# A Mamba-like layer on eight cores: another order at the beginning and at the seam of two passes, and y transposed by TensorE instead of by DMA

## The chip, the cores and the metric

The kernel runs on the eight cores of one Trainium2 chip. Each core works on one batch element of u (4096 rows of 1024 numbers); there is no traffic between cores. The metric is the device time of one execution, in microseconds (us), taken on the slowest core; lower is better. The time of a kernel is the median of its runs.

## The reference, cut to what matters

```python
xn = layernorm(x)                                   # 4096 x 1024 per core
zxbcdt = xn @ in_proj_w.T                           # z 2048, x 2048, B 64, C 64, dt 16
# forward branch, and the same backward in time with its own parameters:
dt  = softplus(dt + dt_bias);  A = -exp(A_log)
xBC = silu(causal_conv4(xBC))
y   = scan(h = h * exp(dt*A) + dt*x*B ;  y = h.C) + D * x      # 16 heads of 128
yz  = y * silu(z)
y_dir = yz * rsqrt(mean(yz*yz) + eps) * norm_w
s = (y_fw + y_bw) @ out_proj_w.T
g = silu(quantize6(xn) @ quantize6(ffn_w).T + ffn_bias)        # blocks of 32, fp6 grid
out = x + s * g
```

## The kernel before

**Two passes.** The sequence is cut into 16 groups of 256 rows, each of two chunks of 128 rows. The first pass (A) goes through the groups from the last to the first. For a group it normalizes u (`layer_norm`), transposes the result by DMA (`xt`), projects it with the weights `wx` (x, B, C; nine blocks) and `wz` (z; four blocks), stores these to memory (`sp_x`, `sp_bc`, `sp_z`), convolves, scans backward and stores y (`sp_y`). It also prepares the quantized input of the FFN (`ffn_input`, stored as `sp_xd`), and once per group for eight groups a tile of the quantized FFN weights (`ffn_weight_tile`). The weights `wx` and `wz` lie as float32 in memory and are cast to bfloat16 by DMAs that GpSimd issues into the large tile `ar`. The second pass (B) goes forward: it loads the spilled x, B, C and z, convolves and scans forward, adds the stored y of pass A (`yb`, a part of `ar`, loaded from `sp_y`), transposes the sum into `yt` (a part of `ar` too), multiplies it by the out-projection weights (`wov`, in `ar`, scaled by `nwt`), computes the FFN (`ffn_chunk`) and writes the output (`b_out`). Between the passes, at the **seam**, `ar` changes hands: `wx` makes way for the FFN weights (`wf`), the bias rows (`fbt`) and the buffers of pass B, `wz` for `wov`. The conv weights (`cd`), `nega`, `ddiag`, `dbt` and others are loaded or made anew for the forward direction.

**What sets the order.** The program is recorded as units (`put` for a compute instruction or a bundle of them, `dma` for a transfer), each with an engine, the units it waits for, and a guess of its duration. `Plan.queues` then runs a list schedule over these guesses: whenever an engine is free it takes, of the units that would be ready, the one with the lowest rank (`P.turn`, or `P.rank` where it is set), then the one recorded first. The result is a fixed order of instructions for each engine. On the chip each engine works through its order; an instruction that has to wait holds up all behind it. All DMAs but those that cast are issued by one queue, SP, in such an order too, and there a wait also holds up all transfers behind it.

**Buffers.** The names in brackets are rings: `Ring.take` hands out the next buffer with the units that must be done before. `ub` (two tiles) holds rows of u, `yz` (three) the gated output, `stg` (five) x for the conv, PSUM is cut into `PJ` (two banks for projections), `CV` (one pair of banks for the conv) and `SC` (two pairs, for the scan's products). All helpers that issue an instruction have one line each: 354 for TensorE, 364 for ScalarE, 367 to 378 for VectorE and GpSimd, 381 for DMAs.

**The places that the change touches.** The constants' DMAs are recorded first, `c_ii` and `cw` ahead of u. VectorE then makes `cd` (six instructions), `nega` and `ddiag` (needs `i128` and `dvt`) before it comes to the statistics of u (`bns`). At the seam sixteen VectorE instructions scale `wov` by `nwt`, and the bias is split into three bfloat16 rows through `stmp` and `yz`. In pass B each chunk's sum of y is transposed by

```python
t_yt = dma("sp", f"yt{yi}", go(yt, yz[:].rearrange("p (k f) -> p k f", k=16),
                              transpose=True), [v, yfree], 512, us=2.4, rate=150.0)
```

## Time and profile before

| | us |
|---|---|
| median of 3 runs | 1624.54 (1620.02 to 1625.74) |
| the profiled execution | 1631.24 |
| its span on the slowest core (5) | 1629.4 |
| TensorE busy in it | 1323.2 |
| VectorE busy | 989.5 |
| ScalarE busy | 826.8 |
| GpSimd busy | 703.0 |

The profile is of one execution; its span is that from the first to the last instruction of the slowest core. PE is TensorE, PEld its weight loads, DVE VectorE, ACT ScalarE, POOL GpSimd, SPq the issuing of DMAs. In a line such as `start us, us, engine line op out<-in xcount [idle before <-releaser]` the brackets say how long the engine stood idle just before and what ended it. The window rows give the busy time of each engine in a stretch, the granted TensorE clock (1.00 is 2.4 GHz, 0.50 is 1.2 GHz), the busy share of the 16 DMA engines and what they moved.

### The profile page before, as it was taken

The numbers are of one execution on the slowest core, as the hardware profiler recorded it, in microseconds if no ns is written. First come the engines' busy times: TensorE is split into PE (matmuls) and PEld (weight loads), VectorE is DVE, ScalarE is ACT, GpSimd is POOL, SyncE is SP. The second block draws the span as 40 slices with busy tenths as digits, with TensorE's granted clock in tenths as the row PEclk, the third lists the DMA queues.
The fourth block names the chain that finished last, engine by engine and source line by source line (L and its number), as shares of the span: only waits on it lengthen the run. The fifth ranks groups of instructions, "written<-read, shape, count | busy, mean of one in ns | idle before, by whom it ended". The sixth has DMA issues, their size and how long they took to land.

```text
span 1629.4 us, 38429 instructions; the slowest of 8 cores (1601.5 to 1629.4 us)
## 1 busy us (share of the span) xinstructions
PE 1323.2 (81%) x13568; PEld 768.9 (47%) x13568; DVE 989.5 (61%) x1769; ACT 826.8 (51%) x1652; POOL 703.0 (43%) x949
## 2 busy tenths in 40 slices
PE   0458989687998899989996379898898988898995
PEld 0325656354655565656663244444444444444442
DVE  1614777665778777667755365666556566565652
ACT  0135656464656566656655354554555555555540
POOL 1422646443555355555532234444443444343442
PEclk9989999898999999999997589998898999999998
DMA  9795889989887687875589777988898899899872
GB/s 163 145 162 94 193 189 202 155 185 194 184 187 155 186 188 180 183 157 145 148 214 261 169 141 172 236 200 203 195 218 191 224 198 226 198 226 206 199 168 77
DMA packets 446831, 298.02 MB, mean 183 GB/s; under 512 B 320689, under 2 KB 394929, under 8 KB 445106
## 3 DMA queue, kind: packets, MB, share of 16 engines
q1 hardware_dynamic: 444050, 282.43, 76.0%
q0 software_dynamic: 2592, 13.14, 5.4%
q8 instruction: 110, 1.80, 0.5%
q14 instruction: 79, 0.65, 0.2%
HBM read 152.39 MB, written 84.93 MB: 146 GB/s over the span
## 4 chain that ended last, share of the span: by engine, by line
PE 51%; DMA 18%; ACT 9%; issue 8%; DVE 8%; SPq 4%; POOL 1%; DVEq 0%; ACTq 0%; POOLq 0%
PE ps L354 51%; SPq L381 4%; DMA xtm<-cvx 4%; ACT L364 3%; DMA ar<-yz 2%; DMA dvt<-dvec 2%; DVE yz L367 2%; DMA g<-scr 2%; ACT e L364 2%; DMA ar<-wob 2%; ACT cvx L364 1%; DMA ar<-wz 1%; ACT sq L364 1%; DMA lts<-spl 1%; DMA xt<-xn 1%
## 5 line engine op out<-in xcount | busy, mean ns | idle before, releaser
L354 PE MATMUL ps<-ar,xt 128*128 128x512 bf16 (+1 forms) x1792 | 382.8, 357 | 134.1 <-DMA xt<-xn 62.4
L354 PEld LDWEIGHTS ps<-ar,xt 128*128 128x128 bf16 x1792 | 149.7, 99 | 328.4 <-issue 186.5
L364 ACT ACTIVATE cvx<-ps,cbt 128x256 bf16<-128x256 f32 x512 | 201.1, 475 | 195.1 <-PE ps L354 157.7
L354 PE MATMUL ps<-xt,ar 128*128 128x256 bf16 x2304 | 276.3, 275 | 11.7 <-DMA ar<-wz 4.2
L354 PE MATMUL ps<-ar 128*128 128x512 bf16 x1024 | 258.6, 397 | 14.2 <-ACT e L364 11.1
L367 POOL TENSOR_TENSOR stmp<-st,dec 128x1024 f32<-128x1024 bf16 x64 | 131.0, 2047 | 277.9 <-DVE spl L378 122.9
L354 PEld LDWEIGHTS ps<-xt,ar 128*128 128x128 bf16 x2304 | 220.0, 99 | 56.0 <-issue 25.6
L367 DVE TENSOR_TENSOR yz<-ps,sz 128x1024 bf16<-128x1024 f32 x128 | 154.9, 1220 | 43.3 <-PE ps L354 42.9
L354 PE MATMUL ps<-stg,cd 64*64 64x256 bf16 x4096 | 156.1, 294 | 24.1 <-ACT cvb L364 12.4
L364 ACT ACTIVATE sq<-yz 128x1024 bf16<-128x1024 bf16 x128 | 135.0, 1054 | 74.0 <-DVE yz L367 35.6
L354 PEld LDWEIGHTS ps<-ar 128*128 128x128 bf16 x1024 | 95.2, 101 | 148.0 <-issue 56.5
L372 POOL TENSOR_SCALAR rr<-rr 128x1 f32<-128x1 f32 x384 | 110.3, 292 | 115.2 <-DVE rr L372 92.9
L367 POOL TENSOR_TENSOR bw<-btm,w 128x1024 bf16<-128x1024 bf16 x64 | 124.5, 1947 | 79.5 <-DMA btm<-cvb 67.1
L354 PEld LDWEIGHTS ps<-stg,cd 64*64 64x64 bf16 x4096 | 113.4, 114 | 80.2 <-issue 76.2
L364 ACT ACTIVATE e<-ps 128x1024 bf16<-128x1024 f32 x128 | 129.6, 1018 | 33.1 <-PE ps L354 32.2
L367 DVE TENSOR_TENSOR e<-e,cbm 128x1024 bf16<-128x1024 bf16 x128 | 97.8, 769 | 58.0 <-ACT e L364 57.9
L371 POOL TENSOR_SCALAR u<-u,stats 128x1024 f32<-128x1024 f32 x32 | 96.9, 3029 | 74.6 <-DVE xn L372 57.8
L354 PE MATMUL ps<-xtm,e 128*128 128x128 bf16 x1024 | 89.6, 233 | 45.0 <-DVE sm L367 16.1
L364 ACT ACTIVATE stg<-ps 128x512 bf16<-128x512 f32 x128 | 76.1, 594 | 94.4 <-PE ps L354 94.0
L364 ACT ACTIVATE sz<-ps 128x512 bf16<-128x512 f32 x128 | 76.4, 598 | 92.7 <-PE ps L354 92.5
L367 POOL TENSOR_TENSOR xd<-v,qs 128x1024 bf16<-128x1024 fp8e4 x40 | 81.7, 2044 | 78.4 <-DMA xd<-xd 32.6
L364 ACT ACT_TABLE_LOAD x66 | 84.7, 1283 | 36.4 <-DMA nega<-alog 18.0
(89 smaller groups left out, 1635.8 us busy)
## 6 DMA issues: line engine op xcount, KB each, us to landing
u<-u SPq DMA_DIRECT2D x54, 512.0 KB, 5.0
sp_x<-stg SPq DMA_DIRECT2D x64, 256.0 KB, 2.8
g<-scr SPq DMA_DIRECT2D x64, 256.0 KB, 5.6
sp_z<-sz SPq DMA_DIRECT2D x32, 512.0 KB, 4.4
sp_y<-yz SPq DMA_DIRECT2D x32, 512.0 KB, 4.8
sz<-sp_z SPq DMA_DIRECT2D x32, 512.0 KB, 4.5
ar<-sp_y SPq DMA_DIRECT2D x32, 512.0 KB, 4.6
stg<-sp_x SPq DMA_DIRECT2D x60, 259.0 KB, 4.8
```

The costliest lines, as they stand in the source:

```text
L354: return lambda e: e.matmul(out, lhsT, rhs, start=start, stop=stop)
L364: return lambda e: e.activation(out, in_, func, **kw)
L367: return lambda e: e.tensor_tensor(out, a, b, op=op)
L371: return lambda e: e.tensor_scalar(out, a, s1, None, op0=op0)
L372: return lambda e: e.tensor_scalar(out, a, s1, s2, op0=op0, op1=op1)
L381: return lambda e: e.dma_start(out=out, in_=in_, **kw)
```

## The change

It has three parts.

1. **The beginning.** u is loaded first, then the constants; `wx` waits for the first tile of u; `i128`, `dvt` and `rh` wait for blocks of `wx`; `wz` starts after `wx` block 5; `ddiag` gets a later rank; the second group's projection (`a_front`) is recorded ahead of the first group's z.
2. **The seam.** The FFN weights (`wf`), the constants of pass B and its first `decays` get an earlier turn or rank; the four loads of `wov` come behind the first loads of pass B, each waits for the one before, and ScalarE scales half of the sixteen slices; the bias is split during pass A through a small tile and a DRAM buffer (`fbd`); tiles of the FFN weights are loaded into the third `yz` buffer in pass A (ring `UM`), so that the ring `yz` has two buffers in pass A and three in pass B.
3. **y.** Sixteen transposes by TensorE (a matmul with the identity `i128` in transpose mode, output bfloat16 in a pair of PSUM banks of the ring `SC`) and two copies of 128x1024 by ScalarE take the place of each DMA transpose.

```diff
-    def dma(self, eng, slot, step, after, kb, us=0.5, rate=180.0):
-        land = 2.0 + kb / rate
+    def dma(self, eng, slot, step, after, kb, us=0.5, rate=180.0, lat=None):
+        land = lat or 2.0 + kb / rate
...
-    YZ = Ring("yz", yzb)
+    YZ = Ring("yz", yzb[:2])
+    UM = Ring("um", [yzb[2][:].bitcast(F32)])
...
+    def tr(out, in_, start, stop):
+        return lambda e: e.matmul(out, in_, i128[:], start=start, stop=stop, is_transpose=True)
...
-    k_ii = dma("sp", "k0", go(ii[:], dr["c_ii"]), [], 16)
-    k_cw = dma("sp", "k5", go(cwt[:], dr["cw"][1]), [], 36)
     t_u0 = []
     for i in range(2):
-        t_u0.append(dma("sp", f"u{i}", go(ub[i][:], dr["u"][L - (i + 1) * Q:L - i * Q, :]), [], 512))
+        t_u0.append(dma("sp", f"u{i}", go(ub[i][:], dr["u"][L - (i + 1) * Q:L - i * Q, :]), [], 512,
+                        lat=6.0 + 2 * i))
+    k_ii = dma("sp", "k0", go(ii[:], dr["c_ii"]), [], 16, lat=8.0)
+    k_cw = dma("sp", "k5", go(cwt[:], dr["cw"][1]), [], 36, lat=9.0)
...
-    for b in (8, 0, 1, 2, 3, 4, 5, 6, 7):
-        k_wx[b] = dma("pool", f"wx{b}", go(wxb[b], dr["wx"][b]), [], 1024, us=1.0, rate=130.0)
+    for n, b in enumerate((8, 0, 1, 2, 3, 4, 5, 6, 7)):
+        k_wx[b] = dma("pool", f"wx{b}", go(wxb[b], dr["wx"][b]), [t_u0[0]], 1024, us=0.6,
+                      lat=4.0 + 3.4 * n)
+    k_i = dma("sp", "k4", go(i128[:], dr["c_i128"]), [k_wx[2]], 32, lat=6.0)
+    k_dv = dma("sp", "k9", go(dvt[:], dr["dvec"][1]), [k_wx[2]], 8, lat=7.0)
+    k_rh = [dma("sp", f"k11{i}", go(rhb[i][:], dr["c_rh"][1, i]), [k_wx[4]], 512, lat=9.0)
+            for i in range(2)]
...
-        k_wz.append(dma("pool", f"wz{b}", go(wzb[b], dr["wz"][b]), [k_wx[7], k_wz[b - 1:b]], 2048,
-                        us=1.0, rate=170.0))
+        k_wz.append(dma("pool", f"wz{b}", go(wzb[b], dr["wz"][b]), [k_wx[7 - 2 * (b == 0)], k_wz[b - 1:b]],
+                        2048, us=0.6, lat=9.5))
...
+        P.rank = P.turn + 1.5
         dd = put("dve", tt(
             ddiag[:], i128[:].unsqueeze(1).broadcast_to([128, NH, 128]),
             dvt[:].unsqueeze(2).broadcast_to([128, NH, 128]), ALU.mult),
-            [k_i, k_dv, after], dve1(2048))
+            [k_i, k_dv, after_dd], dve1(2048))
+        P.rank = None
...
     a_conv(NG - 1, fr[NG - 1])
+    P.turn = 0
+    fr[NG - 2] = a_norm(NG - 2)
+
+    P.turn, P.rank = 2, 0.5
+    a_front(NG - 2, fr[NG - 2])
+    P.turn, P.rank = 1, None
     for c in (1, 0):
         a_z(NG - 1, fr[NG - 1], c)
-    P.turn = 0
-    fr[NG - 2] = a_norm(NG - 2)
-    P.turn = 1
...
-    P.turn = 2 * NG + 1
+    P.turn = 2 * NG
...
-        t_wo.append(put("dve", ts(wov[:, k, :], wov[:, k, :], nwt[:, k:k + 1], ALU.mult),
-                        [k_wo[k // 4], k_nw], dve4(1024)))
...
+            si, sp, sfree = SC.take()
+            tp = sp.bitcast(BF16)
+            p = put("pe", [tr(tp[:, k * 128:(k + 1) * 128], yz[:, k * 128:(k + 1) * 128], k % 8 == 0,
+                              k % 8 == 7) for k in range(16)], [v, sfree, k_i], 0.92)
+            t_yt = [put("act", act(yt[:, h * 8:(h + 1) * 8, :],
+                                   tp[:, h * 1024:(h + 1) * 1024].rearrange("p (k t) -> p k t", k=8),
+                                   AF.Copy), [p, yfree], act_us(1024)) for h in range(2)]
+            SC.give(si, t_yt)
+            YZ.give(sc.yz_i, [p])
...
-    base = P.turn + 1
-    P.turn = base
+    base = P.turn
+    P.rank = base - 0.5
     dcs = {0: decays(0, None, t_par, None)}
+    P.rank = None
     P.turn = base + 1
     front = b_front(0)
+    wov = ar[:, WO:WO + 16384].rearrange("p (k m) -> p k m", k=16)
...
+    for b in range(4):
+        k_wo.append(dma("sp", f"wol{b}", go(
+            wov[:, b * 4:(b + 1) * 4, :], dr["wob"][:, b * 4:(b + 1) * 4, :]),
+            [last_a["wz"], wo_casts, front["loads"], k_wo[b - 1:b]], 1024, lat=6.5))
+        for k in range(b * 4, b * 4 + 4):
+            w_ = wov[:, k, :]
+            if k % 2:
+                t_wo.append(put("act", act(w_, w_, AF.Copy, scale=nwt[:, k:k + 1]),
+                                [k_wo[b], k_nw], act_us(1024)))
```

How the planner's order comes out at three places. First VectorE at the very beginning of the program, before (`cd` are the conv weights, `nega` and `ddiag` parameters of the heads, `bns` the statistics of u, `xn` its normalized rows; s_k5, s_k4 and so on are the semaphores of the constants' loads, s_u0 and s_u1 those of u):

```order
L367 TENSOR_TENSOR cd<-ii,cwt 128x768 [waits s_k5,s_k0]
L367 TENSOR_TENSOR cd<-ii,cwt 128x768 x5
L371 TENSOR_SCALAR nega<-nega 128x32 [waits s_act]
L367 TENSOR_TENSOR ddiag<-i128,dvt 128x2048 [waits s_k9,s_k4]
L454 BN_STATS bns<-u0 128x6 [waits s_u0]
L455 BN_STATS bns<-u0 128x6
L454 BN_STATS bns<-u1 128x6 [waits s_u1]
```

and after:

```order
L475 BN_STATS bns<-u0 128x6 [waits s_u0]
L476 BN_STATS bns<-u0 128x6
L477 BN_AGGR stats<-bns 128x2 [waits s_dve]
L475 BN_STATS bns<-u1 128x6 [waits s_u1]
L476 BN_STATS bns<-u1 128x6
L477 BN_AGGR stats<-bns 128x2 [waits s_dve]
L377 TENSOR_SCALAR xn<-u0,stats 128x1024 [waits s_act]
L372 TENSOR_TENSOR cd<-ii,cwt 128x768 [waits s_k5,s_k0]
L372 TENSOR_TENSOR cd<-ii,cwt 128x768 x5
L376 TENSOR_SCALAR nega<-nega 128x32 [waits s_act]
L377 TENSOR_SCALAR xn<-u1,stats 128x1024 [waits s_xt01]
```

The statistics and the first normalization now stand ahead of `cd`, and `ddiag` has left the place in front of them (it is some thirty instructions further down).

Second the DMA queue SP at the seam, from the last store of pass A on (`ar<-wf` and `ar<-wob` load the FFN and out-projection weights, `lts<-spl` is the first link of pass B's decays), before:

```order
L381 DMA cbt<-cb 128x18
L381 DMA ar<-wf 128x8x1024 [waits s_pe]
L381 DMA ar<-wob 128x4096 [waits s_wo3]
L381 DMA sp_z<-sz1 128x2048 [waits s_act]
L381 DMA ar<-wob 128x4096 x3
L381 DMA xt1<-sp_xd 128x1024 x2
L381 DMA rh0<-c_rh 64x2048 [waits s_pe]
```

and after:

```order
L386 DMA ar<-wob 128x4096 [waits s_wol0]
L386 DMA sz0<-sp_z 128x2048 [waits s_dve,s_szs1,s_szs0]
L386 DMA ar<-wob 128x4096 [waits s_wol1]
L386 DMA sbc0<-sp_bc 128x2x259 [waits s_pe]
L386 DMA sz1<-sp_z 128x2048 [waits s_dve]
L386 DMA ar<-wob 128x4096 [waits s_wol2]
L386 DMA_TRANSPOSE btm0<-cvb0 128x2x128 [waits s_act]
L386 DMA_TRANSPOSE lts0<-spl 128x4x128 [waits s_dve]
```

The four loads of `wob` were issued at one go; now the queue itself stands and waits for each before it issues the next, with `lts` behind the fourth. On VectorE the scaling of `wov` stood ahead of the decays of pass B, and now the decays' instructions on `sm0` and `spl` stand ahead of nearly all of it.

Third TensorE in the middle of pass B (`ar,xt1` is the FFN, `ar` alone the out-projection, `rh,lts` the decay weights of the scan, `on3` the bias; s_yt0 is the landing of the DMA transpose), before:

```order
L354 MATMUL ps<-ar,xt1 128x512 [waits s_act]
L354 MATMUL ps<-ar,xt1 128x512 x6
L354 MATMUL ps<-ar,xt1 128x512 [waits s_yt0]
L354 MATMUL ps<-ar,on3 128x512
L354 MATMUL ps<-ar 128x512 x14
L354 MATMUL ps<-ar 128x512 [waits s_act]
```

and after:

```order
L359 MATMUL ps<-i128,yz1 128x128 x12
L359 MATMUL ps<-i128,yz1 128x128 [waits s_act]
...
L356 MATMUL ps<-ar,xt1 128x512 [waits s_act,s_rh01,s_rh00]
...
L356 MATMUL ps<-rh1,lts0 64x512
L356 MATMUL ps<-ar 128x512 x6
L356 MATMUL ps<-ar 128x512 [waits s_dve]
...
L359 MATMUL ps<-i128,yz2 128x128 x12
L359 MATMUL ps<-i128,yz2 128x128 [waits s_act]
```

The transposes of the two chunks (`i128,yz1`, `i128,yz2`) stand in TensorE's own order, the first ahead of the last FFN half, the second between the two halves of an out-projection, and TensorE waits for VectorE's sums there.

## Rows read from the trace of the kernel before

**Rows 1.** Windows: stretch, length, busy us per engine, PEclk, DMA share, GB/s.

```profile
0.00:62.00 62.00, 0.00 (x0) 0.00 (x0) 16.18 (x28) 2.51 (x6) 15.46 (x24) 1.00 0.86 154
62.00:129.00 67.00, 42.26 (x422) 28.72 (x423) 22.40 (x54) 20.33 (x46) 20.60 (x17) 0.88 0.98 150
129.00:175.00 46.00, 44.31 (x453) 26.81 (x452) 24.31 (x48) 29.21 (x61) 20.05 (x26) 0.95 0.56 135
175.00:873.00 698.00, 622.16 (x6806) 403.53 (x6802) 490.11 (x894) 413.55 (x836) 346.23 (x447) 0.96 0.80 179
873.00:990.00 117.00, 62.41 (x718) 36.41 (x718) 68.10 (x130) 54.54 (x107) 30.66 (x47) 0.68 0.77 183
...
1020.00:1580.00 560.00, 491.55 (x4793) 247.12 (x4794) 338.27 (x579) 287.19 (x561) 241.15 (x341) 0.94 0.91 207
```

**Rows 2.** Chain that ended last, beginning: start us, us, what.

```profile
8.85 32.46 DMA dvt<-dvec
...
43.68 0.69 DVE bns L454
...
55.20 6.99 DMA xt<-xn
62.44 0.58 PE ps L354 x16
```

**Rows 3.** Timeline of VectorE, beginning: the conv weights.

```profile
4.37 5.30 DVE L367 TENSOR_TENSOR cd<-ii,cwt 128x768 bf16<-128x768 bf16 x6 [3.12 <-DMA cwt<-cw]
```

**Rows 4.** Timeline of GpSimd: the last of four loads of wz.

```profile
108.97 0.60 POOL L381 DMA_DIRECT2D ar<-wz  x1
```

**Rows 5.** DMA view, 0 to 125 us: queues (packets, MB, share), one issue group.

```profile
q0 software_dynamic: 1999, 8.85, 47.1%
q1 hardware_dynamic: 19228, 10.44, 43.7%
...
u<-u SPq DMA_DIRECT2D x6, 512.0 KB, 6.8
```

**Rows 6.** The chain that ended last, at the seam.

```profile
876.70 25.19 DMA ar<-wob
...
907.35 4.13 DMA ar<-yz
...
914.38 1.28 ACT L364
...
927.96 3.48 DMA rh<-scr
```

**Rows 7.** Timeline of SP at the seam: the issue of lts.

```profile
916.40 1.23 SPq L381 DMA_TRANSPOSE lts<-spl  x1
```

**Rows 8.** Waits of TensorE, 1000 to 1600 us: total, times, longest.

```profile
PE ps L354 <- DMA ar<-yz: 16.6, 7, 3.1
```

**Rows 9.** Timeline of TensorE in pass B: eight products of 128x128, and the next.

```profile
1276.86 0.61 PE L354 MATMUL ps<-xtm,e 128*128 128x128 bf16 x8 [0.77 <-DVE sm L367]
1277.30 0.36 PE L354 MATMUL ps<-sm,tri 128*128 128x32 f32 x2
```

**Rows 10.** The page: groups of instructions (busy, mean ns of one, idle before).

```profile
L364 ACT ACTIVATE e<-ps 128x1024 bf16<-128x1024 f32 x128 | 129.6, 1018 | 33.1 <-PE ps L354 32.2
...
L354 PE MATMUL ps<-xtm,e 128*128 128x128 bf16 x1024 | 89.6, 233 | 45.0 <-DVE sm L367 16.1
```

**Rows 11.** Tile yz on SP: issue ns, min/median/max of the DMA transposes.

```profile
L381 SPq DMA_TRANSPOSE ar<-yz x32: 1837/3348/5973, 969.0 to 1603.9; - x32
```

**Rows 12.** DMA view, 1596 to 1601 us: the queue of SP.

```profile
q1 hardware_dynamic: 2274, 1.25, 97.2%
```

**Rows 13.** The chain near the end: one DMA transpose of y.

```profile
1596.30 4.46 DMA ar<-yz
```

**Rows 14.** Timeline of VectorE in pass B: the second sum of a group.

```profile
1231.33 1.23 DVE L367 TENSOR_TENSOR yz<-yz,ar 128x2048 bf16<-128x2048 bf16 x1 [6.32 <-DMA ar<-sp_y]
```

**Rows 15.** Timeline of TensorE in the same group: the wait for the first yt.

```profile
1228.71 0.38 PE L354 MATMUL ps<-ar,xt 128*128 128x512 bf16 x1 [2.72 <-DMA ar<-yz]
```

104 lines of the change are left out of this document (49 added, 55 removed).

## The prediction, on record before the changed kernel ran

> **What bounds the kernel now.** I read the windows first, since the kernel has stretches with different limits [rows 1]. In 62 us TensorE does nothing. From 62 to 129 us it is busy 42.26 of 67 us. From 129 to 873 it is busy nearly nine tenths (44.31 of 46, 622.16 of 698): pass A is TensorE's. From 873 to 990, the seam, it is busy 62.41 of 117 us, at a mean granted clock of 0.68, so part of that work ran at 1.2 GHz. From 1020 to 1580, pass B, it is busy 491.55 of 560 us, and there the DMA engines are busy 0.91 of the time, more than in pass A (0.80). So there are three places to look at, and the change has a part in each.
>
> Then the chain of work that ended last, in order of time. At the beginning it is one long step [rows 2]: the transfer of dvt from 8.85 us on, 32.46 us long, on which `ddiag` waits; VectorE works in order, so the statistics of u start only at 43.68 us, though u is small and early in the queue. From there it takes until 62.44 us to the first matmul: two normalizations and two DMA transposes in a row, since `xn` is a single buffer, the second transpose 6.99 us. At the seam the chain holds the load of the out-projection weights, 25.19 us, on which the scaling on VectorE waits, and behind it stand the head parameters, a row of the bias that goes out by a DMA (4.13 us), and only then the decays of pass B; rh, which the first scan needs, is issued at 927.96 and lands 3.48 us later [rows 6]. In pass B the waits of TensorE name the DMA transpose of y seven times, 16.6 us in all [rows 8].
>
> **The change, part by part: the beginning.** u goes first. A load of u takes 6.8 us to land (median, in the crowd of the beginning) [rows 5]; issued at 1 us it lands near 8. From the start of `bns` to the first matmul it was 62.44 - 43.68 = 18.8 us [rows 2], and that is mostly the two normalizations and two transposes, which remain. The six instructions of `cd` (5.30 us [rows 3]) now stand between them, but they fit into the first transpose, which the second normalization waits for anyway (6.99 us for one [rows 2]). A table load of ScalarE of 1.28 us (its size from [rows 6]) now falls into this path. So the first matmul comes at 8 + 18.8 + 1.3 = 28 us, 34 us earlier. From there on the data are the limit. Until 125 us two queues take 47.1% and 43.7% of the 16 engines [rows 5], together 113 us of engine time, and nearly all that they move is still needed before the last block of z weights can be used; a tile of FFN weights (512 KB) comes on top. The last load of `wz` was issued at 108.97 [rows 4] and TensorE went on with it at about 129. With the DMAs packed without the pauses of before, it lands at about 113 - 8 (what belongs to the next groups) = 105 us. That is 24 us earlier. In the meantime the reordered program gives TensorE the second group's projection, a part of which came after 129 us before; that may bring up to 10 us more. From both I take 30 us for the beginning. Bounds: from below, if the transfers give only half of that, 12 us. From above, TensorE's own work until 175 us is 42.26 + 44.31 = 86.6 us [rows 1]; starting at 28 without a wait it would be at the same point at 115, 60 us earlier.
>
> **The seam.** What leaves the path to pass B's decays: the wait for `wob`, the scaling of its slices (now halved too), `ddiag`, the bias and its DMA. The VectorE instructions of pass B's first decays now stand among those of the last scan of pass A, ahead of all but one scaling. But the four loads of `wob` are now each behind a wait in the queue of SP, and the transposes `btm` and `lts` stand behind the issue of the fourth. The last of the four landed 25.19 us after 876.70, together with `wf`, which now goes earlier [rows 6]; so one costs up to 25.19 / 4 = 6.3 us, and three of them and the queue's other waits (the loads of z wait for the last scan) put the issue of `lts` near 873 + 24 = 897. Before it was 916.40 [rows 7], and `rh` followed 11.6 us later. That way stays, so all moves 19 us forward. The scaling that is left lies under these transfers. I take 20 us for the seam; bounds are 8 (if the queue's waits are twice as long) and 40, which is what remains of the 117 us when TensorE's 62.41 us run at full clock and half of the idle goes.
>
> **y on TensorE.** Removed are 32 DMA transposes, each 4.46 us of practically the whole DMA subsystem (alone in its window, 97.2% of 16 engines [rows 12, 13]) and 3.35 us of SP's time in the median [rows 11]. Added are 512 transposes of 128x128. The trace has none; the nearest row is the scan's product with 128 columns and a 128x128 weight load: eight of them from 1276.86 to 1277.30, 0.44 us, 55 ns each [rows 9], though one takes 233 ns by itself [rows 10]. If transposes follow one another in the same way, it is 16 x 0.055 = 0.9 us for a chunk, 28 us for 32. They stand on TensorE, which has only 560 - 491.55 = 68 us free in this stretch [rows 1], so nearly all of it counts. The ends of the price are 0 (all of it in gaps) and 119 us (512 x 233 ns, nothing overlapped). I take the pipelined end, since the 128x128 products of the same shape are. The two copies are like `e<-ps`, 1018 ns each [rows 10], 65 us in all on an engine that is busy half of pass B [rows 1]; they cost nothing where half a product of the FFN stands between the transposes and the out-projection, as it does after the first one in the order shown.
>
> Against the 28 us stand the 16.6 us of waits [rows 8], of which a wait for the sum itself remains. In the group around 1228 us TensorE waited 2.72 us for the first transposed chunk [rows 15]. Now it would transpose at 1224, right after the sum, and go on. But the second sum was late, at 1231.33, after 6.32 us of waiting for `sp_y` [rows 14], because `yb` is one buffer; TensorE now stands before the second transposes until it is there, one to three microseconds. That load was issued behind a transpose on SP, which held the queue for some 3 us [rows 11], so it starts about 2 us earlier. In sum: +28 - 14 (waits) + 5 (waiting for the second sum) - 7 (fewer transfers in a full DMA subsystem) = +12 us. Bounds: -25 and +45.
>
> The page of the Trainium skill on this, "TensorE: Matmul & The Clock Gate", Part 4 (PE-mode transpose), speaks against the change: it gives about 275 ns for a transpose of 128x128 in a kernel and says that in transpose mode the clock gate does not count TensorE as busy. By that it would be 141 us of transposes, and the sum below would end near 1700. In this trace a product of that shape has 233 ns alone and 55 ns in a row; no run here shows a transpose yet.
>
> **Nothing** is expected from the rest: pass A keeps its work, the smaller ring `yz` comes round once in a group, 698 / 14 = 50 us [rows 1], and nothing holds a buffer that long, and at the end 4.46 us of DMA [rows 13] become 0.9 + 2 us of transposes and copies, 1 us less.
>
> **Sum:** -30 - 20 + 12 = -38 us. The profiled execution took 1631.24, so 1593; that one is 6.7 us above the median of the runs, 1624.54, and against it the forecast is 1587.
>
> **Rivals.** (1) *The DMA subsystem was the hidden bound of pass B.* The transposes held it for 32 x 4.46 = 143 us, and the loads of g, y and z wait in that crowd. With them gone pass B gets 15 us shorter instead of 12 longer: 1560. For it speaks the share of 0.91, against it that TensorE is busy 88% (491.55 of 560) with work that remains. (2) *The beginning stays bound by its bytes.* Landing of the last weights moves by 8 us and not 24, since the transfers are as many as before: gain 10, time 1607. For it speaks that they filled 113 of 125 us. (3) *The second transposes wait in every group*, about 3 us for the late sum, 16 times, and the out-projection stands behind them: +28 more in pass B, 1615. (4) The one on the other side: *transposes do not overlap* and take 233 ns each. 119 us instead of 28: 1587 + 91 = 1678. It decides from 130 ns for a transpose on, where the 38 us are eaten up. Against it speaks the spacing [rows 9], for it that no transpose has been seen. (5) *Gains and costs cancel*: both gains at their lower bounds, 20 together, and pass B +20: 1624.
>
> **Chances.** The forecast 0.45, (1) 0.16, (2) 0.14, (3) 0.11, (4) 0.08, (5) 0.06. The range from 1560 to 1616 holds the forecast, (2), (3) and most of (1). A measurement of this kernel tells 0.5%, 8 us, from no change. Faster than that: the forecast, (1), (2) and three quarters of (3), 0.83. Within it: the rest of (3) and most of (5), 0.08. Slower: (4) and the tail of (5), 0.09.
>
> **What the profile will show.** The first matmul at about 28 us; the work that follows the last z weights at about 105; the point that was at 873 at 843; `rh` of pass B's first group about 36 us after that (before 928 - 873 = 55). In pass B sixteen transposes in a row that take about 0.9 us, copies of about 1.02 us, TensorE's busy time up by 28 us, the DMA share below 0.75. The prediction is wrong if transposes cost 130 ns or more, if the last z weights land after 120 us, or if the spacing of groups in pass B changes by more than 2 us.

## The result, and the profile of the changed kernel

The changed kernel takes 1640.45 us in the median (1634.39 to 1642.42) where the kernel before takes 1624.24 beside it: a ratio of 1.0095, 95% interval [1.0064, 1.0126]. The forecast was 1587 us, faster. It is 1% slower, so the direction was wrong and the time lies outside the range. One of its five executions took 1741.08 us, with the cores of one die at a lower granted clock (0.82 to 0.83); such executions, which every kernel has now and then, are left out of all ranges and ratios here. The profiled execution took 1635.97 us with a span of 1634.4.

The same stretches as in [rows 1]: length, busy us per engine, PEclk, DMA share, GB/s.

```profile
0.00:62.00 62.00, 17.33 (x147) 14.61 (x148) 27.92 (x50) 8.25 (x21) 23.65 (x28) 1.00 0.88 168
62.00:129.00 67.00, 46.72 (x397) 28.75 (x395) 14.69 (x33) 20.29 (x41) 15.00 (x15) 0.80 0.97 175
129.00:175.00 46.00, 35.31 (x379) 20.14 (x380) 29.75 (x58) 28.61 (x58) 21.12 (x27) 0.87 0.62 116
175.00:873.00 698.00, 628.62 (x6876) 407.64 (x6876) 496.90 (x914) 421.45 (x854) 354.91 (x456) 0.95 0.83 187
873.00:990.00 117.00, 82.91 (x890) 44.65 (x891) 65.90 (x114) 68.31 (x128) 42.61 (x62) 0.82 0.73 169
...
1020.00:1580.00 560.00, 482.15 (x4821) 254.78 (x4818) 331.02 (x531) 313.06 (x575) 223.18 (x314) 0.95 0.72 171
```

The seam is better filled (82.91 us of TensorE against 62.41). In pass B the DMA share has fallen from 0.91 to 0.72, and yet TensorE gets less done there: 482.15 us against 491.55, though transposes were added to its work.

Windows don't say when a group begins. For that I use one DMA that every group of both passes issues once: `g<-scr`, the decays that come back from memory. On SP, in time order, the first and the last of pass B in the kernel before:

```profile
928.42 1.27 SPq L381 DMA_DIRECT2D g<-scr  x2
...
1548.60 1.22 SPq L381 DMA_DIRECT2D g<-scr  x2
```

and in the changed kernel:

```profile
887.79 1.24 SPq L386 DMA_DIRECT2D g<-scr  x2
...
1549.61 1.23 SPq L386 DMA_DIRECT2D g<-scr  x2
```

At the first group of pass B the changed kernel is 40.6 us ahead; at the last it is 1.0 behind. Pass B alone (fifteen steps of this mark) takes 661.8 us instead of 620.2. Earlier marks split the 40.6: 6.5 at the second group of pass A, 20 more until its last, 14 at the seam.

What TensorE waits for from 1020 to 1560 us (total, times, longest):

```profile
PE ps L356 <- ACT cvb L369: 20.4, 12, 1.9
PE ps L356 <- ACT ar L369: 11.0, 12, 1.1
PE ps L356 <- DVE yz L372: 9.2, 12, 1.5
PE ps L359 <- ACT ar L369: 8.7, 12, 1.9
PE ps L356 <- ACT e L369: 7.6, 6, 1.3
```

The wait for the DMA transpose of y [rows 8] is gone. In its place stand waits for ScalarE: for `ar`, once of the out-projection (L356) and once of the transposes for their PSUM buffer (L359), and above all for `cvb`, the evicted convolution of B and C. (`ar` holds the copies of y, but also other evictions of ScalarE: 3.0 us of the second row remain in e4 below, which has no copies.) That one has nothing to do with y.

The transposes themselves on TensorE (L359), sixteen of one chunk:

```profile
1257.15 1.05 PE L359 MATMUL ps<-i,yz 128*128 128x128 bf16 x16
```

The row runs from the start of the first to the end of the last; one alone takes 219 ns, so from one start to the next it is (1.05 - 0.22) / 15 = 55 ns. They do follow one another closely, as the 128x128 products do [rows 9]. ScalarE's queue around them:

```profile
1258.30 1.94 ACT L369 ACTIVATE ar<-ps 128x1024 bf16<-128x1024 bf16 x2 [0.68 <-PE ps L359]
...
1264.62 1.02 ACT L369 ACTIVATE e<-ps 128x1024 bf16<-128x1024 f32 x1 [0.69 <-PE ps L356]
1268.53 1.28 ACT L369 ACT_TABLE_LOAD   x1 [2.88 <-PE ps L356]
1269.83 0.48 ACT L369 ACTIVATE cvb<-ps,cbt 128x256 bf16<-128x256 f32 x1
1270.20 1.05 ACT L369 ACTIVATE sq<-yz 128x1024 bf16<-128x1024 bf16 x1
...
1271.24 0.47 ACT L369 ACTIVATE cvb<-ps,cbt 128x256 bf16<-128x256 f32 x1
```

and TensorE behind it, with the group before that from 1222 us on:

```profile
1222.66 0.64 PE L356 MATMUL ps<-xtm,bw 128*64 128x128 bf16 x16 [1.27 <-ACT e L369]
...
1225.96 0.40 PE L356 MATMUL ps<-st,gc 64*128 64x128 bf16 x4 [1.89 <-ACT cvb L369]
1226.29 1.92 PE L356 MATMUL ps<-stg,cd 64*64 64x256 bf16 x32
...
1272.05 0.38 PE L356 MATMUL ps<-xtm,e 128*128 128x128 bf16 x4 [1.56 <-ACT cvb L369]
```

The table load stands right in front of the first `cvb`, a square of y between the two `cvb`, and TensorE waits for the second. The windows of 3 us at that place (length, busy TensorE, PEclk, DMA share, GB/s) show a second price (1.00 is 2.4 GHz):

```profile
1223.00:1226.00 3.00, 1.11 (x25) 0.81 0.27 61
1226.00:1229.00 3.00, 3.00 (x45) 0.50 0.05 11
1229.00:1232.00 3.00, 3.00 (x31) 0.55 0.75 252
```

TensorE was busy 1.11 of 3 us, and the work that follows runs at half the clock, 1.2 GHz: the 32 products `stg,cd` take 1.92 us there and 1.07 at full clock. From 1020 to 1500 us the clock falls like this eleven times. Each time a run of short waits stands around it: 1.27 us for `e` and 1.89 for `cvb`, or 0.53 for `yz`, 0.66 for `st` and some 1.5 for `cvb`.

### The profile page after: what moved, and what is told of

It is laid out like the page before. It is cut to its first block, busy times and chain, and to the rows that moved or that the text cites. A ratio compares the mean times of both kernels' runs of the same rounds, so it can differ in the third digit from the quotient of the medians.

```text
span 1634.4 us, 39529 instructions; the slowest of 8 cores (1609.3 to 1634.4 us)
## 1 busy us (share of the span) xinstructions
PE 1357.8 (83%) x14080; PEld 803.4 (49%) x14080; DVE 1009.5 (62%) x1760; ACT 888.5 (54%) x1724; POOL 713.7 (44%) x950
## 4 chain that ended last, share of the span: by engine, by line
PE 51%; DMA 16%; ACT 11%; issue 9%; DVE 7%; SPq 5%; POOL 1%; DVEq 0%; ACTq 0%; POOLq 0%
PE ps L356 50%; SPq L386 5%; DMA xtm<-cvx 3%; DMA ar<-sp_y 2%; ACT ar L369 2%; DMA out<-u 2%; DMA xt<-xn 2%; ACT sq L369 2%; ACT e L369 2%; DVE yz L372 1%; ACT L369 1%; ACT cvx L369 1%; DMA lts<-spl 1%; ACT cvb L369 1%; DMA g<-scr 1%
## 5 line engine op out<-in xcount | busy, mean ns | idle before, releaser
L356 PE MATMUL ps<-ar,xt 128*128 128x512 bf16 (+1 forms) x1792 | 382.0, 356 | 99.0 <-DMA xt<-xn 45.4
L356 PE MATMUL ps<-xt,ar 128*128 128x256 bf16 x2304 | 278.4, 278 | 23.8 <-ACT cvb L369 6.9
L356 PEld LDWEIGHTS ps<-ar,xt 128*128 128x128 bf16 x1792 | 150.0, 99 | 293.6 <-issue 152.3
L356 PE MATMUL ps<-ar 128*128 128x512 bf16 x1024 | 250.8, 387 | 25.0 <-DVE ost L372 6.9
L356 PEld LDWEIGHTS ps<-xt,ar 128*128 128x128 bf16 x2304 | 222.6, 100 | 68.3 <-issue 36.7
L372 POOL TENSOR_TENSOR stmp<-st,dec 128x1024 f32<-128x1024 bf16 x64 | 134.5, 2102 | 213.0 <-DVE st L372 148.7
L356 PE MATMUL ps<-stg,cd 64*64 64x256 bf16 x4096 | 161.9, 300 | 24.9 <-ACT cvx L369 8.4
L356 PEld LDWEIGHTS ps<-ar 128*128 128x128 bf16 x1024 | 92.0, 99 | 153.9 <-issue 67.3
L369 ACT ACTIVATE ar<-ps 128x512 bf16<-128x512 f32 (+1 forms) x128 | 100.2, 809 | 119.5 <-PE ps L356 93.3
L377 POOL TENSOR_SCALAR rr<-rr 128x1 f32<-128x1 f32 x384 | 118.6, 314 | 96.9 <-DVE rr L377 80.6
L356 PEld LDWEIGHTS ps<-stg,cd 64*64 64x64 bf16 x4096 | 116.3, 117 | 81.0 <-issue 76.5
L369 ACT ACTIVATE e<-ps 128x1024 bf16<-128x1024 f32 x128 | 129.8, 1018 | 40.9 <-PE ps L356 40.4
L369 ACT ACTIVATE sz<-ps 128x512 bf16<-128x512 f32 x128 | 76.6, 598 | 99.7 <-PE ps L356 99.4
L356 PE MATMUL ps<-xtm,e 128*128 128x128 bf16 x1024 | 91.7, 238 | 23.7 <-ACT cvb L369 10.5
```

The costliest lines, as they stand in the source:

```text
L356: return lambda e: e.matmul(out, lhsT, rhs, start=start, stop=stop)
L369: return lambda e: e.activation(out, in_, func, **kw)
L372: return lambda e: e.tensor_tensor(out, a, b, op=op)
L377: return lambda e: e.tensor_scalar(out, a, s1, s2, op0=op0, op1=op1)
```

## The experiments

All ratios are to the kernel before, run beside each kernel. Differences of ratios are turned into us at 1620 us for the whole. "Pass B" is the distance from the first to the last `g<-scr` of pass B in the one profiled execution, "pass A" that from its second to its last group. Five kernels with DMA transposes of y and otherwise different edits have 614.4 to 621.6 us in pass B, so a difference of 7 us in it means little.

| run | ratio [95% interval] | pass A | pass B |
|---|---|---|---|
| before | 1 | 687.9 | 620.2 |
| changed | 1.0095 [1.0064, 1.0126] | 667.6 | 661.8 |
| e1, y by DMA, rest changed | 0.9840 [0.9799, 0.9880] | 672.3 | 614.7 |
| e2, y on TensorE, rest as before | 1.0224 [1.0173, 1.0274] | 685.0 | 666.2 |
| e3, copies on VectorE | 0.9869 [0.9831, 0.9907] | 663.3 | 625.9 |
| e4, transposes, no copies | 0.9662 [0.9628, 0.9696] | 677.6 | 592.2 |
| e5, copies planned at 0.01 us | 0.9955 [0.9917, 0.9993] | 661.1 | 645.2 |
| e6, one copy each | 0.9804 [0.9776, 0.9832] | 658.7 | 630.1 |
| e9, copies of 8 columns | 0.9966 [0.9926, 1.0006] | 667.2 | 645.0 |
| e13, one copy each, planned at 0.01 | 0.9981 [0.9950, 1.0012] | 665.0 | 634.4 |
| e15, order of e3, copies on ScalarE | 0.9965 [0.9943, 0.9987] | 663.4 | 638.6 |
| e17, order of e3, one copy each | 0.9906 [0.9871, 0.9940] | 660.5 | 636.4 |
| e16, e4 with transposes doubled | 0.9747 [0.9708, 0.9785] | 662.5 | 612.2 |

### Which part costs: e1 and e2

e1 puts this back into the changed kernel; e2 puts the other form into the kernel before.

```diff
...
-            p = put("pe", [tr(tp[:, k * 128:(k + 1) * 128], yz[:, k * 128:(k + 1) * 128], k % 8 == 0,
-                              k % 8 == 7) for k in range(16)], [v, sfree, k_i], 0.92)
-            t_yt = [put("act", act(yt[:, h * 8:(h + 1) * 8, :],
-                                   tp[:, h * 1024:(h + 1) * 1024].rearrange("p (k t) -> p k t", k=8),
-                                   AF.Copy), [p, yfree], act_us(1024)) for h in range(2)]
...
+            t_yt = dma("sp", f"yt{yi}", go(yt, yz[:].rearrange("p (k f) -> p k f", k=16),
+                                          transpose=True), [v, yfree], 512, us=2.4, rate=150.0)
...
```

> The changed kernel with only its third part undone: y is transposed by DMA again. Theory T (the third part costs what pass B lost, some 42 us between its first group, where the changed kernel was 41 us ahead, and the end): 1640 - 42 = about 1598 us, and the steps of pass B are again 42.2 us from group to group, not 45.1. Rival S (the 42 us belong to something else in pass B that the first two parts bring, such as the ring of buffers for u, or to a bound that takes back any head start): within 8 us of 1640, steps still 45 us.

> The kernel before with the third part alone (y transposed by TensorE, copied by ScalarE). Theory T: 1624 + 42 = about 1666 us, with 2.9 us more for each of the groups of pass B and nothing changed before 880 us. Rival S: within 8 us of 1624. Rival R (the third part only costs much when pass B runs with the seam's new order): between the two, near 1640.

Theory T holds in e1: 0.9840, and pass B is 47 us shorter. The third part costs 1.0095 - 0.9840 = 2.6%, 41 us. In e2 it costs 2.2%, 36 us, and pass B 46 us. The first two parts bring 26 us, and pass B does not give them back.

### Copies: e3 and e4

e3 makes both copies on VectorE:

```diff
-            t_yt = [put("act", act(yt[:, h * 8:(h + 1) * 8, :],
+            t_yt = [put("dve", cp(yt[:, h * 8:(h + 1) * 8, :],
...
-                                   AF.Copy), [p, yfree], act_us(1024)) for h in range(2)]
+                        [p, yfree], 1.0) for h in range(2)]
```

e4 has the transposes and no copy (`z_yt` is a memset that puts a constant in `yt`, so y is left out of the output):

```diff
-            t_yt = [put("act", act(yt[:, h * 8:(h + 1) * 8, :],
...
-            SC.give(si, t_yt)
+            t_yt = [p, yfree, z_yt]
+            SC.give(si, [p])
```

> The changed kernel with both copies of each transposed y on VectorE, not on ScalarE. Theory A (the 1.94 us of two copies stand in ScalarE's queue ahead of exponentials and of the activation for the convolution, and TensorE waits for those): the 32 x 1.94 us leave ScalarE, the wait of PE for ACT in pass B falls from about 49 us towards the 36 us of before; if VectorE has room for them (it is busy 62% of the span), 1605 to 1625 us. Theory B (TensorE's own time and the PSUM buffer of the transposes are the cost): within 6 us of 1640. Theory C (VectorE's queue is as tight, so that the copies late there hold up the sums and decays): above 1646.

> The changed kernel with its transposes on TensorE, but without the copies out of PSUM: the out-projection multiplies a constant in place of y, so the output is not that of the reference. Theory A (ScalarE's copies are the cost): about 1600 to 1610 us. Theory B (TensorE's transposes, 29.5 us busy in pass B, and their wait for the sum): about 1630 us, since only the wait of the out-projection for the copy goes. If both share it, between 1610 and 1630.

Both beat what was expected. With the copies on VectorE the kernel is at 0.9869; without any it is at 0.9662, under even the low end of theory A. So transposes alone make the kernel faster than DMA transposes, by 29 us (0.9840 - 0.9662), and everything is lost with the copies: 70 us from e4 to the changed kernel, though they are 62 us of work on an engine that is busy little more than half of pass B. Pass B from 1020 to 1500 us in e1, then in e4:

```profile
1020.00:1500.00 480.00, 419.38 (x4109) 211.22 (x4106) 294.23 (x506) 250.84 (x492) 206.00 (x289) 0.94 0.92 212
```

```profile
1020.00:1500.00 480.00, 438.30 (x4712) 231.41 (x4710) 316.18 (x525) 263.93 (x515) 222.05 (x312) 1.00 0.76 194
```

In e4 TensorE keeps its full clock throughout; in e1 the clock falls twelve times in this stretch: four times at a wait for the transposed y (2.3 to 2.6 us), six at one for `sm` (1.65 us) and two at one for `spl` (1.48 us), both of the decays. Over all of pass B TensorE is busy for 525.96 us in e4 and 529.77 in e1, though e4 has the transposes on top: at a mean clock of 0.98 against 0.92 they cost no busy time in sum, and the idle time is 66.2 us against 84.9.

VectorE's copy is also the shorter one. Duration min/median/max in ns, in e3 on VectorE and in e15 (below) on ScalarE:

```profile
L383 DVE COPY ar<-ps x64: 674/682/692, 932.9 to 1577.8; 128x1024 bf16<-128x1024 bf16 x64
```

```profile
L406 ACT ACTIVATE ar<-ps x64: 1006/1024/1031, 935.6 to 1592.8; 128x1024 bf16<-128x1024 bf16 x64
```

This is as the Trainium skill has it on "VectorE: DVE Perf Modes", Why PSUM operands drop a tier: a bf16 copy out of PSUM may still run at two elements a cycle, f32 at one. In e20 (below) the same copy moves 512 f32 in place of 1024 bf16 and takes 684 ns, so the trace agrees:

```profile
L383 DVE COPY ar<-ps x32: 677/684/692, 952.2 to 1588.0; 128x512 f32<-128x512 f32 x32
```

### Order against work: e5, e6, e9

The planner weighs every unit by a planned duration. Two planned copies therefore move PE's and ScalarE's other operations too. These three tell the two apart.

e5 keeps the copies and changes their planned length:

```diff
-                                   AF.Copy), [p, yfree], act_us(1024)) for h in range(2)]
+                                   AF.Copy), [p, yfree], 0.01) for h in range(2)]
```

e9 keeps the planned length and the order, and copies one column of each 128 (the rest of `yt` is a constant, so most of y is left out of the output):

```diff
-            t_yt = [put("act", act(yt[:, h * 8:(h + 1) * 8, :],
-                                   tp[:, h * 1024:(h + 1) * 1024].rearrange("p (k t) -> p k t", k=8),
+            t_yt = [put("act", act(yt[:, h * 8:(h + 1) * 8, 0:1],
+                                   tp[:, h * 1024:(h + 1) * 1024].rearrange("p (k t) -> p k t", k=8)[:, :, 0:1],
```

e6 copies the first half on ScalarE and the second on VectorE:

```diff
...
+                    put("dve", cp(yt[:, 8:16, :], tp[:, 1024:2048].rearrange("p (k t) -> p k t", k=8)),
+                        [p, yfree], 1.0)]
```

> The changed kernel with every copy still on ScalarE, but planned at 0.01 us instead of 1.03 us each, so that the planner puts PE's and ScalarE's other work nearly in the order of the run without copies (1566 us): both activations for the convolution of B and C stand together again, the exponentials of the decays behind the first out-projection. Theory O (the order that the planned copies bring about is the cost, the table load in front of the activation on the path): 1580 to 1600 us. Theory W (the 62 us of copy work on ScalarE are the cost, whatever the order): within 8 us of 1635. Rival L (copies in a queue planned without them come late and hold up more): above 1645.

> The changed kernel with the first half of each y copied by ScalarE and the second by VectorE at the same time, so that the PSUM buffer is free one copy sooner. The planned order is again near that of the run without copies. Theory O: 1580 to 1595 us, better than both copies on VectorE (1600). Theory W: half way between 1600 and 1635, near 1618.

> The changed kernel in its own order, with the copies planned at full length, but each copying 8 columns in place of 1024 (the rest of the transposed y is a constant, so the output is not that of the reference). With the last runs this makes a table of two orders by two amounts of ScalarE work. Theory O: 1620 to 1635 us, since the order stays. Theory W: 1566 to 1575 us, since the work is gone.

e5 lands between O and W: another order with all of the work brings 1.4%, 23 us. e9 is no better: the same order without the work brings 1.3%, 21 us, and not the 65 or more of theory W. Its `cvb` wait stayed at 20.1 us, as the order says. e6 is as theory O has it, 0.9804. Neither theory alone holds; but e5's order was not quite that of e4, so the table is not clean.

### The order held fixed: e15, e17, e16

e15 and e17 plan the copies on VectorE, as e3, and then move their units into ScalarE's queue at their planned start, both or the first only. All else stands as in e3 on PE, ScalarE and VectorE.

```diff
...
+            if getattr(u, "to", u.eng) != u.eng:
+                order[u.eng].remove(i)
+                u.eng = u.to
+                q = order[u.eng]
+                q.insert(sum(begun[j] <= begun[i] for j in q), i)
...
```

> The changed kernel with both copies on ScalarE at full length, while every other operation of PE, ScalarE and VectorE stands exactly in the order of the run with the copies on VectorE (1600 us, pass B at granted clock 1.00): the copies' units are planned for VectorE and then moved into ScalarE's queue at their planned start. The changed kernel itself (1636 us on this chip) differs from it in order alone. Theory O (the order is most of the cost): 1595 to 1608 us. Theory W (the copies' place on ScalarE is most of it, whatever the order): 1625 to 1640 us. Both half: near 1617.

> As the first of this call, in the same order, but only the first half of each y copied by ScalarE, the second by VectorE. Theory O: the place of the copies hardly counts in this order, so within 6 us of the version with both on VectorE (1600) and of the first of this call, a little below both since the PSUM buffer is free sooner: 1590 to 1600 us. Theory W: 1615 us.

e15 comes out at 0.9965, the case "both half". With the work the same, the changed kernel's order costs 1.0095 - 0.9965 = 1.3%, 21 us, and 23 us in pass B. With the order the same, copies on ScalarE and not on VectorE cost 1.0%, 16 us; e17 lies between (0.9906), though a little above the 1600 us expected. Waits of TensorE in e15, same window as above:

```profile
PE ps L379 <- DVE yz L395: 23.0, 18, 2.1
PE ps L379 <- DVE rr L399: 16.3, 12, 1.4
PE ps L379 <- ACT ar L406: 11.4, 12, 1.1
PE ps L379 <- ACT spl L392: 11.1, 12, 0.9
```

and in e3:

```profile
PE ps L356 <- DVE yz L372: 27.7, 23, 2.3
PE ps L356 <- DVE rr L376: 13.5, 12, 1.2
PE ps L356 <- ACT spl L369: 11.1, 12, 0.9
PE ps L356 <- DVE ar L383: 4.4, 11, 0.5
```

The wait for `cvb` is not among them. ScalarE's queue in e15 shows why: both `cvb` stand in one row, and TensorE needs them only 3.7 us after the first begins.

```profile
1131.92 1.28 ACT L392 ACT_TABLE_LOAD   x1 [0.41 <-PE ps L379]
1133.22 0.84 ACT L392 ACTIVATE cvb<-ps,cbt 128x256 bf16<-128x256 f32 x2
```

```profile
1136.93 0.28 PE L379 MATMUL ps<-cvb 128*128 128x128 bf16 x2
```

Between e3 and e15 the copies' own wait grows from 4.4 to 11.4 us and the one for `rr` from 13.5 to 16.3, while the one for `yz` falls by 4.7. These rows show where the copies are in the way; they don't account for all of the 16 us.

The two prices look different over the whole of pass B, from its first to its last `g<-scr` (length, busy us per engine, PEclk, DMA share, GB/s). The changed kernel, e15, e3:

```profile
887.79:1549.61 661.82, 555.54 (x5655) 294.50 (x5648) 394.15 (x642) 367.85 (x685) 260.17 (x365) 0.94 0.71 168
```

```profile
892.83:1531.39 638.56, 532.73 (x5644) 279.13 (x5706) 383.58 (x646) 376.51 (x690) 262.86 (x367) 0.98 0.71 174
```

```profile
890.71:1516.58 625.87, 537.37 (x5712) 278.34 (x5706) 418.04 (x703) 325.42 (x634) 262.37 (x367) 0.98 0.74 178
```

TensorE is idle for 106.3 us in the changed kernel and for 105.8 in e15. So the 23 us between these two orders are not more waiting in sum: the waits for `cvb` are gone in e15, but others stand in their place. What differs is the busy time, at a mean clock of 0.94 against 0.98. (e15's trace lacks some 60 matmuls by its count of weight loads; at 0.09 us each that makes 17 to 23 us, an estimate.) Nor is it one execution: the mean clock of a core lies between 0.932 and 0.947 in the changed kernel and between 0.949 and 0.965 in e15, over four and ten executions. From e3 to e15 it is the other way round. The clock stays, and the idle time grows from 88.5 us to between 100 and 106: copies on ScalarE cost waiting.

Two kernels double the transposes of e4. e14 plans them at double length and so gets a new order, e16 at the old length:

```diff
-                              k % 8 == 7) for k in range(16)], [v, sfree, k_i], 0.92)
+                              k % 8 == 7) for k in list(range(16)) * 2], [v, sfree, k_i], 0.92)
```

> The kernel with transposes and no copies (1566 us; the out-projection multiplies a constant) with every transpose made twice, 1024 instead of 512. This measures the price of the transposes by itself. If TensorE's own time sets the pace of pass B and 16 transposes take 0.99 us: +32 us, 1598. If they fall into waits that are there anyway: +5 to 15 us. If they cost 233 ns each without overlap: +119 us.

> The kernel with transposes and no copies (1566 us), every transpose made twice, but planned at the old length, so that all the rest stands in the same order (the last version with doubled transposes also changed the order, and took 114 us more). It leaves out the copies, so the output is not that of the reference. If TensorE's own time sets the pace, 16 more in 0.99 us at full clock, 32 times: +32 us, 1598 us. If 233 ns each without overlap: 1685 us, and the 114 us were the transposes'. If they fall into waits: 1571 to 1580 us.

e14 took 1679.87 us in its profiled execution, pass B 711.5, as if 233 ns each without overlap were true. But `cvb` was back among TensorE's waits (22.2 us) and 32 transposes in a row took 1.95 us at full clock, so they did overlap: 16 more in a row are 1.95 - 1.05 = 0.90 us more (0.99 in the expectations is a little too much). e16, with the order of e4 and the same number of transposes, is at 0.9747: 14 us over e4, 20 in pass B. So 512 more transposes cost about 14 to 20 us here, half to two thirds of their 32 x 0.90 = 29 us, and the other 100 us of e14 were order. That the first 512 cost the same is taken over from this, not shown.

Two attempts at a better version failed to be one: e13 is e6 with both copies planned at 0.01 us, e20 is e6 with each copy as pairs of bf16:

```diff
...
+            y4 = yt.rearrange("p k t -> p (k t)").bitcast(F32)
+            t_yt = [put("act", act(y4[:, 0:512], sp[:, 0:512], AF.Copy), [p, yfree], act_us(1024)),
+                    put("dve", cp(y4[:, 512:1024], sp[:, 512:1024]), [p, yfree], 1.0)]
```

> The changed kernel with one copy on ScalarE and one on VectorE (1592 us), planned at 0.01 us each, so that the rest stands as in the run without copies. If order and work both count, as the last runs say, and the split alone already gives the better order: 1580 to 1592 us. If only the work counts now: 1592 us. If copies planned without length come late and hold others up, as one version with both on ScalarE (1617) may have it: above 1600.

> The changed kernel with one copy on ScalarE and one on VectorE (0.980 of the kernel before), in exactly the same order, but each copy moves pairs of bf16 as 512 f32 instead of 1024 bf16. ScalarE's evictions of 128x512 f32 take 0.60 us where its copies of 128x1024 bf16 take 0.97, so 12 us of ScalarE's work go; VectorE's copies stay at 0.68. If ScalarE's work at this place counts as in the fixed order (moving 62 us of it away was worth 16 us): 3 to 8 us, 0.976. If what is left is order and waits for sums alone: no change, 0.980.

e13 has steps of 51 and 36 us in turn where e6 has about 42; planned without length, the copies made a worse order (0.9981). e20 has e6's order and copies with 0.37 us less on ScalarE: 0.9848 [0.9810, 0.9887], not below e6. Its pass B, 625.5 us, is 5 shorter, within what pass B varies by, and its pass A, which the edit doesn't touch, came out 25 longer. Nothing is gained that these runs can tell.

### The beginning: e10, e11, e18

In the changed kernel the first normalised x was ready early but its transpose was late: start and length in the chain, and the first matmul.

```profile
10.96 29.43 DMA xt<-xn
```

```profile
44.67 0.57 PE L356 MATMUL ps<-ar,xt 128*128 128x16 bf16 x16 [44.67 <-DMA xt<-xn]
```

Before, such a transpose took 6.99 us [rows 2]. Now nine weight loads were issued just ahead, from 6.1 to 10.3 us, and the last of them landed 31.8 us after its issue. e10 (on e1) holds six of them back:

```diff
-    for n, b in enumerate((8, 0, 1, 2, 3, 4, 5, 6, 7)):
+    for n, b in enumerate((8, 0, 1)):
         k_wx[b] = dma("pool", f"wx{b}", go(wxb[b], dr["wx"][b]), [t_u0[0]], 1024, us=0.6,
                       lat=4.0 + 3.4 * n)
...
+    for n, b in enumerate((2, 3, 4, 5, 6, 7)):
+        k_wx[b] = dma("pool", f"wx{b}", go(wxb[b], dr["wx"][b]), [fr[NG - 1]["xt"][2]], 1024, us=0.6,
+                      lat=4.0 + 3.4 * n)
```

> The kernel with y transposed by DMA and the other two parts of the change (1594 us), with a beginning in which only three of the nine blocks of in-projection weights are loaded at once; the other six, and what follows them, wait for the landing of both transposes of the normalised x. Theory Q (the first transpose took 29 us because it stood behind nine weight loads): it lands some 18 us after the start instead of 40, the first matmul comes near 20 us, and with six blocks of 3 to 3.4 us each still to land from about 22 us, the kernel ends 10 to 18 us sooner, 1576 to 1584 us. Rival Y (all the weights' bytes have to land before the stage moves on, whatever the order): within 5 us of 1594. Rival X (a DMA transpose takes long at that time for another reason): the transpose still lands after 35 us, and the kernel is slower, above 1600.

The first matmul:

```profile
27.25 0.57 PE L356 MATMUL ps<-ar,xt 128*128 128x16 bf16 x16 [27.25 <-DMA xt<-xn]
```

That is the 28 us of the prediction; the first transpose now takes 12.97 us behind three loads. The ratio is 0.9791 [0.9734, 0.9849], which overlaps e1's (its three times lie far apart, 1583.79, 1595.15 and 1601.52 us), and the second group of pass A stands at 158.6 us against e1's 156.3: 17 us won at the first matmul are gone 130 us later. The waits of TensorE in e10 up to 175 us say where they went:

```profile
PE ps L356 <- DMA xt<-xn: 30.6, 3, 27.3
PE ps L356 <- ACT cvb L369: 22.2, 2, 20.5
PE ps L356 <- DMA ar<-wx: 7.5, 3, 5.3
```

One wait of 20.5 us and three for weights took their place. The trace shows what stands behind that one wait. ScalarE's first `cvb` (75.14 us) stands in its queue behind the statistics of the next group; those wait for a load of u that SP issues at 58.73, and SP's queue had stood until 56.45 for another DMA transpose, that of the FFN's input, now in the crowd of the six loads:

```profile
30.42 25.97 DMA xd<-xd
```

And the last load of z weights, which the first group needs, lands at 119.9 us in e10 as in e1 (110.10 + 9.8, 108.82 + 10.9). So Q is right on the transpose and Y on the time. How much of that landing is bytes and how much the order of GpSimd's queue is open.

e11 takes out the changed beginning as a whole, on e1: the loads stand in the order of the kernel before, and `a_front(NG - 2)` behind `a_z(NG - 1)`.

> The kernel with y transposed by DMA (1594 us) with its beginning put back too (the loads of the kernel before, and the next group's in-projection behind the first z); the weight tiles of the gate's projection in their own buffer and the new seam stay. Theory G (the beginning is worth what its landmarks show, some 6 us): 1600 us. Theory H (it is worth more, because groups 5 to 15 run better behind it): 1610 to 1614 us. Rival N (the landmarks of two profiles of the old beginning differ by 7 us from each other, so it is worth nothing): within 3 us of 1594.

e11 is at 0.9889 [0.9843, 0.9936]: 0.5% over e1, with overlapping intervals. At the second group its beginning, the old one, stands at 158.4 us, two others of the old one at 161.8 and 154.3, the changed one in fifteen executions at 148.8 to 164.0, the median 157.3. The beginning's worth is some 8 us by the ratios and 1 by the marks, and nothing is within what both vary by.

e18 puts the beginning of e10 into e6.

> The changed kernel with one copy on each of ScalarE and VectorE (1592 us), and with the beginning in which six of nine weight blocks wait for the first transposes. If that beginning is worth what the two ratios say (0.979 against 0.984, though their intervals overlap): 1584 us. If the bytes bound the beginning: within 4 us of 1592.

0.9847 [0.9798, 0.9895], not below e6's 0.9804.

### The tiles' buffer and the seam: e12, e19

e12 loads the tiles of the FFN weights (the gate's projection, in the expectation's words) into the buffers of u again, on e1:

```diff
-    YZ = Ring("yz", yzb[:2])
-    UM = Ring("um", [yzb[2][:].bitcast(F32)])
+    YZ = Ring("yz", yzb)
...
-        mi, u, mfree = UM.take()
+        ui, u, mfree = U.take()
```

> The kernel with y transposed by DMA (1594 us), with the weight tiles of the gate's projection loaded into the two buffers for u again, and three buffers for the gated y in both passes. Theory V (the 15 to 20 us that pass A gained between its groups 1 and 15 come from the tiles' own buffer): 1608 to 1614 us, with the lost time at the groups in which tiles are loaded (2 to 10). Rival K (they come from the beginning or from the order): within 4 us of 1594. Rival M (the third buffer for the gated y, missing in pass A until now, helps more than the tiles' buffer): below 1590.

e19 puts the seam back, on e1. Its edit is the seam's part of the diff in reverse: the four loads of `wob` and the scaling of all sixteen slices on VectorE ahead of `conv_weights` and `head_params`, the bias by three small DMAs.

> The kernel with y transposed by DMA (0.984 of the kernel before), with the seam put back too: the weights of both projections are loaded and scaled by VectorE ahead of pass B's constants, as before. The beginning and the tiles' own buffer stay. Theory L (the seam is worth the 14 us that its landmarks show): 0.9925, some 1608 us. The prediction's own size: 20 us, 0.996. Rival P (pass B gives the head start back): within 4 us of 1594.

e12: 0.9883 [0.9847, 0.9918], 0.4% over e1. Its pass A is 687.9 us, as the two kernels without the buffer have it (687.9 and 685.0), while those with it have 658.6 to 684.1, the median 665. Theory V fits the length of pass A, 15.6 us over e1's; but only 7 us are seen in the whole time, with overlapping intervals, and 10.7 of the 15.6 are lost in the last five steps (steps of 51 us at 11, 13 and 15), not where the tiles are loaded. e19: 0.9900 [0.9856, 0.9944], 0.6% over e1, 10 us, again with overlapping intervals. From the last group of pass A to the first of pass B it is 77.5 us, with 78.8 and 76.6 in the two other kernels with the old seam, and 62.0 to 68.8 in all with the new one. These marks make it the clearest of the three. The three parts, 8, 7 and 10 us, add up to the 26 that e1 has, though each by itself is near the noise.

## Why the prediction was wrong, by its steps

**Copies on ScalarE at nothing: the step that failed.** The prediction put 65 us of copies on ScalarE at nothing, because half a product stands between the transposes and the out-projection and the engine is half idle. Their duration was right (1019 ns in the changed kernel against 1018 from [rows 10]). But ScalarE takes its queue in order, and so does TensorE behind it. From e4 to e15, 0.9662 to 0.9965, the copies cost 3.0%, 49 us, although the order is not quite the same; from e4 to e3, on VectorE, 2.1%, 34 us. Shown with the order fixed are 16 us between the two engines; how the 34 us on VectorE divide into work and the small difference of order is open, as no kernel had e4's own order with copies.

**The order was not priced at all.** The prediction counted on everything else staying, and looked at the order only where transposes and out-projection stand. The planned copies also moved the activation of B and C behind a table load, with a square between its halves: 20.4 us of waits and a lower clock behind them. The whole of the order, the changed kernel against e15, is 21 us, and in pass B it comes out as lower clock (0.94 against 0.98) and not as more idle time. How much of it is due to `cvb` alone no run separates.

**The transposes.** 0.9 us for sixteen was predicted, from spacings of 55 ns; measured are 0.90 us for sixteen more in a row (1.05 for sixteen with the end of the last). That step was right. The price of 512 more is 14 to 20 us and not 28, so a part falls into waits. Rival (4) is refuted. The Trainium skill ("TensorE: Matmul & The Clock Gate", Part 4) gives about 275 ns for one; here it is 219 ns for one and 56 ns for each more in a row, at a granted clock of 1.00 in e4 and e16, and the measurement decides. Whether a transpose counts for the clock no run here tells, because other work surrounds it.

**+12 for y on TensorE** becomes, in sum: -29 (e1 to e4: transposes in place of DMA transposes, the clock with them) + 49 (e4 to e15: copies) + 21 (e15 to the changed kernel: order) = +41 us; the first two terms hold differences of order too. The upper bound, 45, held it. The second sum's lateness, rival (3), is there but small: 9.2 us of waits for `yz` from 1020 to 1560 us. (Its own working does not come out: 16 waits of 3 us are 48 us, 43 more than the 5 in the sum, and not 28.) Rival (1) was half right: without copies the kernel is faster than with DMA transposes. It isn't shown that the freed DMA engines did this. VectorE's wait for `sp_y` from 1020 to 1560 us is 67.5 us before, 59.2 in the changed kernel and 38.7 in e4, but such a load takes as long as before to land (median 4.7 us before, 4.8 in e4).

**The beginning, -30.** Two steps failed. The transpose of x was taken at its old 6.99 us while the change put nine loads ahead of it; it took 29.43. And the last load of z weights was to land at 105 us, but was issued at 110.31 and landed 9.7 us later, at 120.0: 9 us sooner than before (108.97 + 19.7 = 128.7) and not 24. More than that, e10 reached the 28 us for the first matmul and won nothing certain by it. Rival (2), bound by the transfers, has this landing nearly to the microsecond (8) and came nearest in the gain: 10 us, where e11 finds some 8 and the marks less.

**The seam, -20.** Right in mechanism: `g<-scr` of pass B's first group comes 14 us sooner after pass A's last, and e19 gives 10 us. It is the size that was half of what was forecast.

**Nothing from the rest** was wrong to the good: pass A is some 20 us shorter. The likely cause, argued more than shown, is that the tiles left the buffers of u, for which e12 finds 7 us in the whole time.

Together the first two parts bring 26 us (e1) where 50 were forecast, and the third costs 41 where 12 were forecast: 15 us in place of -38.

**The better kernels.** e1, e6 and e10 all beat both: 0.984, 0.980 and 0.979. Their intervals overlap, so none is called the best. e6 keeps y on TensorE and differs from the changed kernel by one copy in two on VectorE and by the order that follows.

## What to carry to other kernels

An eviction on an engine that is half idle isn't free: price it by what stands behind it in that engine's queue, and by which engine copies this type fastest. Where a planner sets the order, an added operation moves all the others; compare the order of the whole group first, and test a part with the order held fixed, since two orders of the same work differed here by 21 us, and by some 100 in e14, where the operation in question cost 14 to 20. Look at the granted clock beside the waits: the idle time of two orders can be equal and their busy time not. An earlier first matmul is worth only what the next mark in the profile keeps of it.

## What the runs showed that was not expected

A DMA transpose issued right behind nine loads of weights took 29.43 us, one behind three 12.97 (e10), and 6.99 after all nine had landed [rows 2].

TensorE's granted clock depended on the order of the program. It was 1.00 from 1020 to 1500 us in e3, e4, e15 and e16, 0.94 in e1, and 0.95 in the changed kernel, which does the same work as e15 in another order. In e15:

```profile
1020.00:1500.00 480.00, 410.91 (x4328) 214.59 (x4383) 293.57 (x489) 285.52 (x523) 207.35 (x288) 1.00 0.74 183
```

Its TensorE is busy 410.91 us here and 409.22 in the changed kernel, and yet it gets through 4328 matmuls against 4134 (by the records of the traces, a few of which can be missing).
